# Minus the row maxima written into the score banks by ScalarE in place of a row product on TensorE

## The reference

```
scores = einsum('bhqd,bhkd->bhqk', q, k) * scale        # scale 1/8, 1024 x 1024 per head and batch
attn = softmax(scores, axis=-1)
out = einsum('bhqk,bhkd->bhqd', attn, v)
out = out.transpose(0, 2, 1, 3).reshape(b, s, H * DH) @ w_out.T + residual
```

## Time and profile before

| | |
|---|---|
| median of 3 runs | 917.42 us |
| the profiled execution's own time | 909.34 us |
| its span, first to last instruction | 907.6 us |
| mean granted TensorE clock | 0.946 |
| PE busy | 818.4 us (90%) |
| DVE busy | 641.9 us (71%) |
| ACT busy | 394.1 us (43%) |
| POOL busy | 663.3 us (73%) |

### The profile page before, as it was taken

How to read it: one execution, slowest core, us unless ns; L and a number is a source line. 1 busy time by engine, 2 the same in 40 slices (tenths; PEclk the granted TensorE clock), 3 DMA queues, 4 the chain that set the end, 5 groups by cost and what they waited for, 6 DMA issues and landing times.

```text
span 907.6 us, 14678 instructions
## 1 busy us (share of the span) xinstructions
PE 818.4 (90%) x5118; PEld 489.8 (54%) x5118; DVE 641.9 (71%) x1156; ACT 394.1 (43%) x644; POOL 663.3 (73%) x350
## 2 busy tenths in 40 slices
PE   3678999999999999999999999999999977959591
PEld 1435555555555555555555555555555434448581
DVE  7877777777777777777777777777777767536023
ACT  2443444444444444444444444444444324326351
POOL 3684988888878787878788787878778866532433
PEclk8776999999999999999999999999999989869796
DMA  7200001010101010101011111010010100068693
GB/s 194 79 1 13 13 13 25 13 25 14 24 14 25 14 25 13 24 14 24 14 24 14 25 13 25 13 26 14 13 13 13 24 13 1 13 211 273 212 328 88
DMA packets 84330, 43.91 MB, mean 48 GB/s; under 512 B 57632, under 2 KB 73376, under 8 KB 84192
## 3 DMA queue, kind: packets, MB, share of 16 engines
q1 hardware_dynamic: 83232, 40.86, 17.6%
q0 software_dynamic: 1024, 2.10, 0.7%
HBM read 36.51 MB, written 6.16 MB: 47 GB/s over the span
## 4 chain that ended last, share of the span: by engine, by line
PE 78%; DVE 7%; DMA 5%; POOL 5%; issue 2%; ACT 1%; SPq 1%; POOLq 0%; DVEq 0%; ACTq 0%
PE ps_o L445 25%; PE ps_m L411 9%; PE ps_x L399 8%; PE ps_s L429 6%; PE ps_s L431 6%; PE ps_s L435 6%; PE ps_s L433 6%; PE ps_s L462 3%; DMA moe<-xs_dram 3%; PE ps_s L453 3%; POOL xs_dram L944 2%; DVE mx L1082 1%; PE ps_s L578 1%; PE ps_s L587 1%; DMA wu<-in_wqk 1%
## 5 line engine op out<-in xcount | busy, mean ns | idle before, releaser
L930 POOL TENSOR_TENSOR acc<-acc,probs 128x1024 f32<-128x1024 f32 (+1 forms) x192 | 459.7, 2394 | 80.4 <-ACT probs L684 58.0
L1082 DVE TENSOR_REDUCE mx<-ps_m 128x2 f32<-128x1024 f32 x240 | 293.8, 1224 | 92.8 <-PE ps_m L411 92.0
L684 ACT ACTIVATE probs<-ps_s 128x1024 f32<-128x1024 f32 x256 | 248.9, 1023 | 162.8 <-PE ps_s L435 162.8
L445 PE MATMUL ps_o<-probs,c_all 128*64 128x512 f32 x1024 | 249.7, 608 | 0.0
L930 POOL TENSOR_TENSOR acc<-probs 128x1024 f32<-128x1024 f32 (+1 forms) x32 | 75.2, 2351 | 57.5 <-ACT probs L684 56.9
L429 PE MATMUL ps_s<-q_hi,k_hi 64*128 64x512 f32 x512 | 103.1, 399 | 12.0 <-DVE x_sb L1135 12.0
L445 PEld LDWEIGHTS ps_o<-probs,c_all 128*64 128x64 f32 x1024 | 62.4, 136 | 93.2 <-issue 44.3
L411 PE MATMUL ps_m<-k_hi,q_hi 64*128 64x512 f32 x480 | 108.1, 446 | 3.7 <-DVE mx L1082 3.7
L431 PE MATMUL ps_s<-q_hi,k_lo 64*128 64x512 f32 x512 | 101.8, 394 | 0.0
L435 PE MATMUL ps_s<-neg_row,one_row 64*128 64x512 f32 x512 | 101.6, 393 | 0.0
L433 PE MATMUL ps_s<-q_lo,k_hi 64*128 64x512 f32 x512 | 101.0, 390 | 0.0
(11 more groups left out here) (289 smaller groups left out, 1034.2 us busy)
## 6 DMA issues: line engine op xcount, KB each, us to landing
probs<-in_experts SPq DMA_DIRECT2D x15, 578.0 KB, 5.4
rr<-rd_dram SPq DMA_DIRECT2D x62, 128.0 KB, 3.0
wu<-in_wqk SPq DMA_DIRECT2D x16, 256.0 KB, 3.1
neg_row<-nm SPq DMA_DIRECT2D x256, 0.5 KB, 2.0
w_first<-in_experts SPq DMA_DIRECT2D x5, 578.0 KB, 4.6
rot<-in_experts SPq DMA_DIRECT2D x5, 578.0 KB, 5.1
hT<-in_experts SPq DMA_DIRECT2D x5, 578.0 KB, 5.6
xs_dram<-zero SPq DMA_DIRECT2D x2, 960.0 KB, 6.8
```

Source lines behind the costliest of these rows:

```text
L445: ins = nc.tensor.matmul(ps_o[64 * h:64 * h + 64, :], c_all[:, (p // HP) * TB + kt, :], probs[:, st % 4, h, :], start=(kt == 0), stop=(kt ...
L684: nc.scalar.activation(probs[:, st % 4, :, :], ps_s[:, 2 * (st % 2):2 * (st % 2) + 2, :], ACT.Exp, scale=SCALE).then_inc(s["probs"], 1)
L930: V.tensor_tensor(acc[:, half, heads, :], first, probs[:, st % 4, heads, :], ALU.add).then_inc(s["added"], 1)
L1082: V.reduce_max(mx[:, :, kh, qt], max_banks(q, n), AX.X).then_inc(s["max_reduced"], 1)
```

## The change

The row product is taken out. `neg_wide` holds minus the maxima on all 128 partitions, one tile for each half and head. ScalarE copies it into a step's two score banks (`preset`), and the three products are added to what stands there. A preset stands directly behind the exponential that read the same banks: in ScalarE's order E(2g), preset 2g + 2, E(2g + 1), preset 2g + 3. Steps 1 and 9 are set at the head of groups 0 and 4, behind the copy of the denominators and ahead of the group's first exponential, since `denominators` and `outputs` use their banks. The waits that `score` had pass to `preset`.

The maxima now go out to DRAM in one DMA per half and come back in two, spread over the partitions. `neg_max` waits for the store, `max_spread` for the store and for the last preset that read the tile. The tiles `one_row` and `neg_row` and their clears are gone. In TensorE's order the second value product of every group stands behind the denominators and outputs of groups 3 and 7 instead of ahead of them. Only the first of the four output products of a half carries the start flag.

```
-                ge(pe, s["probs"], n_step(p, st) - 2)
-                if kt == 0:
-                    pe.wait_ge(row_placed[half], 128 * (p + 1))
-                if kt == 1:
-                    ge(pe, s["den_read"], n_part(p, half) - 2)
-                    ge(pe, s["out_added"], n_part(p, half) - 3)
+                pe.wait_ge(s["preset"], n_step(p, st))
...
-                    nc.tensor.matmul(bank[h], k_hi[rows(h), p % 3, kc], q_hi[rows(h), p % 3, qc], start=True, stop=False)
+                    nc.tensor.matmul(bank[h], k_hi[rows(h), p % 3, kc], q_hi[rows(h), p % 3, qc], start=False, stop=False, skip_group_check=True)
...
-                for h in range(2):
-                    ins = nc.tensor.matmul(bank[h], one_row[rows(h), :], neg_row[rows(h), p % 2, qc], start=False, stop=True)
...
-                                           g_all[:, p // HP, p % HP, :], start=True, stop=True)
+                                           g_all[:, p // HP, p % HP, :], start=(n == 0), stop=(n == 3))
...
-                    for n in (2 * g - 2, 2 * g - 1):
+                    def value_step(n):
                         if n >= 0:
                             pv(p, n)
                         elif p > 0:
                             pv(p - 1, NSTEP + n)
+
+                    value_step(2 * g - 2)
                     if g in (3, 7):
                         pe.wait_ge(s["probs"], n_step(p, 2 * g + 1))
...
                         outputs(p - 1, 1, ps_s[:, 3, :])
+                    value_step(2 * g - 1)
...
+            def preset(p, st):
+
+                half, kt = divmod(st, TB)
+                if p == 0 and st < 2:
+                    act.wait_ge(s["max_reduced"], NMAX - 1 + st)
+                ge(act, s["probs"], n_step(p, st) - 2)
+                if kt == 0:
+                    act.wait_ge(row_wide[half], 32 * (p + 1))
+                if kt == 1:
+                    ge(act, s["den_read"], n_part(p, half) - 2)
+                    ge(act, s["out_added"], n_part(p, half) - 3)
+                nc.scalar.copy(ps_s[:, 2 * (st % 2):2 * (st % 2) + 2, :], neg_wide[:, half, :, :]).then_inc(s["preset"], 1)
...
                     if g == 0 and p > 0:
                         den_out(p - 1, 0, ps_s[:, 2, :])
+                        preset(p, 1)
                     if g == 4 and p > 0:
                         den_out(p - 1, 1, ps_s[:, 2, :])
+                    if g == 4:
+                        preset(p, 9)
...
                     expo(p, 2 * g)
+                    if g < NGRP - 1:
+                        preset(p, 2 * g + 2)
+                    elif p < LAST:
+                        preset(p + 1, 0)
                     expo(p, 2 * g + 1)
+                    if g not in (3, NGRP - 1):
+                        preset(p, 2 * g + 3)
...
-                if q >= 2:
-                    sp.wait_ge(s["scores"], n_step(q - 2, TB * half + TB - 1))
+                sp.dma_start(mr_dram[half].rearrange("h (t p) -> p h t", p=P), nm[:, half, :, :],
+                             allow_slow_non_contiguous=True).then_inc(row_out[half], 16)
+
+            def max_spread(q, half):
+
+                sp.wait_ge(row_out[half], 16 * (q + 1))
+                if q:
+                    sp.wait_ge(s["preset"], n_step(q - 1, TB * half + TB - 1))
                 for h in range(2):
-                    for n in range(4):
-                        row = neg_row[64 * h:64 * h + 1, q % 2, half * HALF + n * P:half * HALF + (n + 1) * P]
-                        sp.dma_start(row.bitcast(F32), nm[:, half, h, n:n + 1].bitcast(F32)).then_inc(row_placed[half], 16)
+                    sp.dma_start(neg_wide[:, half, h, :],
+                                 mr_dram[half, h:h + 1, :].to_broadcast([P, HALF])).then_inc(row_wide[half], 16)
```

More of the change, by code:

```diff
@@ L91, in build @@
         hi_of, lo_of = (q_hi, k_hi), (q_lo, k_lo)
-        one_row = sb("one_row", [P, P], F32R)
-        neg_row = sb("neg_row", [P, 2, S], F32R)
+        neg_wide = sb("neg_wide", [P, 2, 2, HALF])
         probs = sb("probs", [P, 4, 2, HALF])
@@ L96, in build @@
         mx = sb("mx", [P, 2, 2, TB])
-        nm = sb("nm", [P, 2, 2, 4], F32R)
+        nm = sb("nm", [P, 2, 2, 4])
         den = sb("den", [P, HALF])
@@ L107, in build @@
         rt_sb = sb("rt_sb", [P, 12, TB * E])
+        mr_dram = nc.dram_tensor("mr_dram", [2, 2, HALF], F32, kind="Internal").ap()
         rd_dram = nc.dram_tensor("rd_dram", [2, 2, HALF], F32, kind="Internal").ap()
@@ L206, in build @@
             "max_row": "both heads' maxima of half the queries, negated (vector)",
-            "scores": "both heads' scores of a step, less the maximum (tensor)",
+            "preset": "a step's score banks hold minus the maximum (scalar)",
+            "scores": "both heads' scores of a step, added to it (tensor)",
             "probs": "their probabilities (scalar)",
@@ L245, in build @@
         up_in = sem("up_in")
-        row_placed = [sem(f"row_placed{n}") for n in range(2)]
+        row_out = [sem(f"row_out{n}") for n in range(2)]
+        row_wide = [sem(f"row_wide{n}") for n in range(2)]
         den_cols_in, inv_out, inv_in = sem("den_cols_in"), sem("inv_out"), sem("inv_in")
@@ L428, in score @@
                 for h in range(2):
-                    nc.tensor.matmul(bank[h], k_hi[rows(h), p % 3, kc], q_hi[rows(h), p % 3, qc], start=True, stop=False)
+                    nc.tensor.matmul(bank[h], k_hi[rows(h), p % 3, kc], q_hi[rows(h), p % 3, qc], start=False, stop=False, skip_group_check=True)
                 for h in range(2):
-                    nc.tensor.matmul(bank[h], k_lo[rows(h), p % 3, kc], q_hi[rows(h), p % 3, qc], start=False, stop=False)
+                    nc.tensor.matmul(bank[h], k_lo[rows(h), p % 3, kc], q_hi[rows(h), p % 3, qc], start=False, stop=False, skip_group_check=True)
                 for h in range(2):
-                    nc.tensor.matmul(bank[h], k_hi[rows(h), p % 3, kc], q_lo[rows(h), p % 3, qc], start=False, stop=False)
-                for h in range(2):
-                    ins = nc.tensor.matmul(bank[h], one_row[rows(h), :], neg_row[rows(h), p % 2, qc], start=False, stop=True)
+                    ins = nc.tensor.matmul(bank[h], k_hi[rows(h), p % 3, kc], q_lo[rows(h), p % 3, qc], start=False, stop=True, skip_group_check=True)
                 ins.then_inc(s["scores"], 1)
@@ L747, in exp_logits @@
                 nc.scalar.activation(rt[b][:, 1, :], rt[b][:, 0, :], ACT.Exp).then_inc(s["logit_exp"], 1)
+            preset(0, 0)
+            preset(0, 1)
             for p in range(NPAIR):
@@ L991, in then @@
                 dve.wait_ge(s["vector_step"], seq[0])
[L993 to L997, removed]
+            V.memset(ones[:], 1.0).then_inc(s["constants"], 1)
             def statistics(src, tiles):
@@ L1085, in neg_max @@
                 dve.wait_ge(s["max_reduced"], NMAX * q + TB * (half + 1))
-                ge(dve, row_placed[half], 128 * q)
+                ge(dve, row_out[half], 16 * q)
                 V.tensor_reduce(nm[:, half, :, :], mx[:, :, :, 4 * half:4 * half + 4].rearrange("p h k t -> p h t k"),
@@ L1409, in _ @@
             weights(2)
-            sp.wait_ge(s["constants"], 1)
-            max_rows(0, 0)
-            max_rows(0, 1)
+            for half in range(2):
+                max_rows(0, half)
+                max_spread(0, half)
             weights(3)
@@ L1416, in _ @@
                 if p > 0:
-                    if p < LAST + 1:
-                        max_rows(p, 1)
+                    max_rows(p, 1)
+                    max_spread(p, 1)
                     den_cols(p - 1, 0)
@@ L1423, in _ @@
                     max_rows(p + 1, 0)
+                    max_spread(p + 1, 0)
                 if p > 0:
```

## The result

| | before | after |
|---|---|---|
| median of 4 runs each | 917.69 us | 1156.48 us |
| lowest to highest | 915.74 to 919.55 | 1155.36 to 1157.42 |
| span, granted TensorE clock | 907.6 us, 0.946 | 1153.6 us, 0.868 |

What follows compares the result with a forecast made beforehand. PE was taken to bound the kernel, 78% of the chain. About −1 us over 15 pairs and +2.4 in the last gave some +1.5, so 911 profiled; adding 8.1 for the runs' median gave 919 us, range 890 to 945.

Steps and rivals of the forecast that it cites:

- Queues: On SP's queue, the 1024-element store lands in 2.5 us (1.8 to 5), leaving the denominators' columns on time.
- rival D: On SP's queue, a store over 4 us stalls DVE's reciprocal twice a pair; at 5 us, 948 us; chance 0.06.
- The reciprocal due at 12.3: DVE's reciprocal is due 12.3 us after group 3's first maxima start; its columns land by 10 to 10.5.
- M(7): Group 3's second maxima on PE start 1.89 us after its first, behind DVE's reduction and a weight load.
- M(8): First maxima of group 4, after group 3's denominators: at 7.38 us against 6.97, +0.41, twice a pair.
- a plain group: Group without denominators, six a pair: 4.87 us; removal gains 0.16, not 0.46, because the maxima's DVE round trip ends last.
- the wait ahead of the denominators: In groups 3 and 7, PE stands 0.47 us for the second exponential, which is queued behind a preset.
- The last pair: Final pair of heads, no maxima or up products: +0.7 for ACT, +1.3 for scores, +0.4 before last outputs; +2.4 together.
- A: In plain groups the DVE round trip does not bind: six groups at 4.57 us a pair, 890 total; chance 0.17.
- B: ACT's serial exponentials and presets bound each group once preset plus hand-over passes 1.37 us; 960 at 1.5; chance 0.12.
- C: DVE's divide meets a POOL add, taking 2.12 us instead of 0.68: +43 us, 940 with half caught; chance 0.12.
- E: On ACT a preset takes 0.92 us and step 9's scores do not stall: 912 us, inside the forecast's 0.53.

Runs made afterwards that it cites:

- e1: Kernel before, plus small constant stores to DRAM in six shapes at the end of each half's SP round, unawaited except by the next of their kind; 923.76 us.
- e2: Kernel before, plus the change's store (of a constant) and SP's wait for it behind the row transfers; 1228.29 us against 911.46.
- e12: e2 with the store's 1024 elements placed 64 B apart in DRAM; 1000.63 us against 917.0 for the kernel before.
- e5: Changed kernel, maxima made for every fourth query by a stepped weight load, so the store goes in 16 B runs with a plain preset; 938.16 us against 912.03.
- e9: Changed kernel, maxima gathered in SBUF by eight small transfers, stored in 2 KB runs behind the columns, broadcasts after the denominators' round; 913.05 us, ratio 1.0003.
- e10: e9 with VectorE's maxima reductions over only 256 of each 512 keys; 885.47 us, ratio 0.9707 to the kernel before.
- e11: e9 with one preset per half moved behind the second exponential of groups 3 and 7; 899.40 us, ratio 0.9857 to the kernel before.
- e4: Changed kernel, maxima stored in 16 B runs and put in order by the preset reading with a 16 B step; 1111.87 us, ratio 1.219 to before.
- e6: e5 with each group's first value product moved between the scores and the second maxima; 964.03 us, ratio 1.0576 to the kernel before.
- e8: Kernel before with only the first value product moved between the scores and the second maxima; 970.77 us, ratio 1.0657.
- e3: Changed kernel with the wait for the store and the broadcasts moved behind the denominators' round on SP's queue; 956.21 us, ratio 1.046 to before.

## Why the prediction was wrong

**The step that failed** is the store in "Queues": "this one has 1024 elements, so I take 2.5 (1.8 to 5)". It landed in 8.7, outside its own bounds. The nearest row, 1.8 for `rd_dram<-rc` of the same 4 KB, writes runs of 32 B; this store writes 4 B at a time, word beside word (e1: 2.5 against 8.8 to 11.2). I widened the bound for the count of elements, which e1 shows to be the wrong quantity. The loss follows from this term, by the rule that I had written beside it ("gone if the store takes over 4 us", rival D): e2 reproduces the loss from the store alone, e12 takes most of it back by the place of the words alone.

**The price of D** was too small beyond its landing. By its own rule 8.7 gives (8.7 − 4) × 30 = 141 us. Two things were missing. The columns, behind two broadcasts, land 4.3 us (the median; 4.9 in the stretch shown) after their issue and not 2.1, so that the reciprocal was late by 6.2 and PE stood 5.7 of it, 29 × 5.7 = 165 us. In e5, with the same order and a quick store, they land in 3.2, so only half of that delay comes from the order; the other half stays open. And the halved clock after the stall, 2.5 us and 0.3 in the next group, makes 29 × 2.8 = 81 us more, 246 in all; "a clock under 1.00 in mid-run" was held unlikely because PE would stay busy, which no longer held.

**The reciprocal due at 12.3** was right: 437.56 − 6.21 − 419.13 = 12.2.

**What was right**, on the after kernel's own timeline, counted from 419.13: M(7) at 1.91 (forecast 1.89), up at 2.34 (2.33), E(7)'s end 4.27 (4.28), denominators 4.31 (4.40), the preset 1.02 (1.06), M(8) at 7.42 (7.38), a plain group 4.88 (4.87). With the store out of the way e9 comes out at +0.5 us against a forecast of +1.5. That the row product's 59 us would bring only a third of themselves, because R frees the maxima's banks last, is shown by e10; that the wait ahead of the denominators eats that third, by e11.

**The last pair** was forecast at +2.4. From the start of the last negated maxima to the end of the span, before has 907.6 − 734.6 = 173.0 us and e9 912.0 − 732.6 = 179.4, so +6.4, while the loop between the first and the last of them is 3.7 shorter than before, not 0.6. These two terms are off in opposite ways, by +4.0 and −3.1, so that e9's total comes so near the forecast is in part luck. I did not take either apart; single executions differ by some us.

**The rivals.** A does not hold (4.88, not 4.57), but e10 shows its price to be right: 27.6 us for what was booked as 29. B's mechanism is real at a preset of 2.05 (e4), at about the price that B gave it, and far off at 1.02. C's is real too (e6, e8), but not at this change's phase: the divides' mean is 799 ns after, 846 in e9, against 794 before. E's preset of 0.92 did not come.

## What to carry to other kernels

Before a DMA is put on a queue ahead of something with a due time, look at how its elements lie in the target: a store that writes single 4-byte words side by side is another kind of transfer than one with runs, and it must be measured, not read off the nearest row by bytes. A wait that such a transfer brings costs its excess over the slack, what lands later behind it, and the clock lost to the stall. And where a matmul is removed, follow the buffer that the engine reuses: the gain here was set by a reduction, and where one preset of ScalarE stood decided whether the gain was kept. The profile did not name that reduction as what was waited for; shortening it did.

## What the runs showed of the hardware

- A 4 KB store to DRAM: 8.8 to 11.2 us word beside word, with neighbours from different partitions, 5.7 to 6.6 with words 8 B apart within 64 B of one partition, 3.4 to 3.8 at 64 B apart, 2.4 to 4.3 in runs of 16 or 32 B (e1).
- A transfer issued 2.1 us behind the slow store, which lands in 2.1 alone, was there after 7.6 (e3).
- ACT's copy of 128x1024 into PSUM takes 1.02, as the exponential out of it does; with a source step of 16 B 2.05 (e4).
- A weight load with a step of four elements takes 305 ns, against 184 (e5).
- A divide of VectorE beside GpSimd's add takes 1.93 (e8) or 2.07 us (e6, both medians) in place of 0.68, and a reordering of TensorE alone brought 26 and 27 of the 31 there.
